# Layer 0's message sum: GpSimd's weighing is made to wait for VectorE's one-hots, and ScalarE makes the one-hots of every fourth group

## The reference, cut to what matters

```
        k_rel = jnp.einsum('nhd,rhde->rnhe', k, rel_att)
        v_rel = jnp.einsum('nhd,rhde->rnhe', v, rel_msg)
        key_e = k_rel[edge_type, edge_src]
        val_e = v_rel[edge_type, edge_src]
        att = (q[edge_dst] * key_e).sum(-1) * rel_pri[edge_type] / jnp.sqrt(jnp.float32(dk))
        ...
        w = ex / denom[seg]
        hsum = jax.ops.segment_sum(w[:, :, None] * val_e, seg, num_segments=S)
        cnt = jax.ops.segment_sum(jnp.ones((seg.shape[0],), x.dtype), seg, num_segments=S)
        t_rel = hsum.reshape(n, r, out_dim)
        present = cnt.reshape(n, r) > 0
        nrel = jnp.maximum(present.sum(-1), 1).astype(x.dtype)
        t = (t_rel * present[..., None].astype(x.dtype)).sum(1) / nrel[:, None]
```

## Time and profile before

| | us |
|---|---|
| median of 3 runs | 4695.33 |
| the 3 runs | 4687.55 to 4701.94 |
| the profiled execution | 4699.63 |
| its span, first to last instruction | 4697.9 |
| the sum's stretch, from the first one-hots (2364.1) to the last addition (2943) | 579 |

### The profile page before, as it was taken

The page is one execution under the profiler, slowest core; times in us unless marked ns, Lnnn a source line. Parts: engine busy times, 40 slices in busy tenths (PEclk is TensorE's granted clock), DMA queues, the critical chain, the costliest instruction groups (busy, mean ns, idle before and its releaser), DMA issues. The chain is left out here.

```text
span 4697.9 us, 56406 instructions
## 1 busy us (share of the span) xinstructions
PE 2830.0 (60%) x10793; PEld 1814.8 (39%) x10794; DVE 3034.3 (65%) x6076; ACT 1521.1 (32%) x3846; POOL 2074.6 (44%) x2102
## 2 busy tenths in 40 slices
PE   0799997666666665000077777666455566655653
PEld 0455554434334333000055555344234444444442
DVE  5333334555555555899889999666456666666657
ACT  0122222333333332322023333333243344334444
POOL 1000004777777776000033333222277777777751
PEclk9999998677776777555599999799677777777776
DMA  5344447999999998100056655000266666666652
GB/s 155 105 141 142 139 135 241 315 313 315 317 314 313 315 315 275 32 0 0 22 197 202 200 197 196 20 18 17 51 174 189 190 193 194 186 190 192 193 155 89
DMA packets 648049, 815.94 MB, mean 174 GB/s; under 512 B 155094, under 2 KB 552310, under 8 KB 647602
## 3 DMA queue, kind: packets, MB, share of 16 engines
q1 hardware_dynamic: 532228, 457.32, 30.5%
q0 software_dynamic: 115696, 357.28, 25.1%
HBM read 541.33 MB, written 274.25 MB: 174 GB/s over the span
## 5 line engine op out<-in xcount | busy, mean ns | idle before, releaser
L821 POOL DMA_INDIRECT rows<-kv,kvi x880 | 832.2, 946 | 889.6 <-DVEq L893 621.8
L1721 POOL DMA_INDIRECT g_rows<-x1t,srci x880 | 847.6, 963 | 286.8 <-issue 257.8
L866 PE MATMUL psD<-qs,hot 128*128 x1760 | 692.9, 520 | 271.1 <-DVE prod L907 201.9
L907 DVE TENSOR_TENSOR prod<-rows,psD 128x256 f32<-128x256 f32 x880 | 367.2, 418 | 458.8 <-DMA rows<-kv,kvi 335.5
L1875 PE MATMUL g_psM<-g_rows,g_hot 128*128 128x264 f32 x1760 | 567.7, 477 | 77.4 <-DVE g_rows L1993 68.1
L1157 POOL TENSOR_TENSOR wv<-vrows,wgt 128x1024 f32<-128x1024 f32 x110 | 217.4, 1976 | 839.0 <-DMA vrows<-val_v 598.8
L866 PEld LDWEIGHTS psD<-qs,hot 128*128 128x128 f32 x1760 | 382.5, 251 | 528.5 <-issue 312.6
L1237 PE MATMUL psM<-wv,vhot 128*128 128x260 f32 x1760 | 444.9, 396 | 137.5 <-DVE run L1256 130.7
L1875 PEld LDWEIGHTS g_psM<-g_rows,g_hot 128*128 128x128 f32 x1760 | 388.0, 232 | 170.7 <-issue 94.5
L886 ACT ACTIVATE off<-psB,npiota 128x256 f32<-128x256 f32 x440 | 207.8, 472 | 668.1 <-PE psB L857 666.8
L1237 PEld LDWEIGHTS psM<-wv,vhot 128*128 128x128 f32 x1760 | 317.5, 190 | 264.8 <-DVE run L1256 218.4
(11 more groups left out here) (364 smaller groups left out, 4629.7 us busy)
## 6 DMA issues: line engine op xcount, KB each, us to landing
val_v<-rows SPq DMA_DIRECT2D x220, 512.0 KB, 5.2
vrows<-val_v SPq DMA_DIRECT2D x220, 512.0 KB
kv<-stage SPq DMA_DIRECT2D x98, 768.0 KB, 4.7
sums_v<-g_run SPq DMA_DIRECT2D x110, 528.0 KB, 3.6
g_drow<-drow_v SPq DMA_DIRECT2D x55, 512.0 KB
rows<-kv,kvi POOLq DMA_INDIRECT x880, 4.9
g_rows<-x1t,srci POOLq DMA_INDIRECT x880
g_ndt<-nodeb SPq DMA_DIRECT2D x440, 6.0 KB
```

Of the source, the lines that this page charges most:

```text
L821: nc.gpsimd.indirect_dma_start(out=rows[:, k], out_offset=None, in_=table, in_offset=bass.IndirectOffsetOnAxis(ap=index[:, i * SLOTS + k:i ...
L866: nc.tensor.matmul(psD[:, k % 4, 0:cols], hot[:, t % 2, j * P:(j + 1) * P], node[:, ds(blk[t], 1)].rearrange("p o d -> p (o d)"), start=Tr ...
L907: ins = nc.vector.tensor_tensor(prod[:, k % 4], rows[:, k, 0:D], psD[:, k % 4, 0:D], ALU.mult)
L1721: nc.gpsimd.indirect_dma_start(out=rows[:, i % NBUF, k, 0:ROW1], out_offset=None, in_=dr["x1t"], in_offset=bass.IndirectOffsetOnAxis(ap=v[ ...
```

## The change

Three edits, all in `sum_messages`:

- **GpSimd** waits, ahead of each weighing, for `hot_done`: for group 1 until VectorE has made the one-hots of groups 0 and 1 of the same turn, for group 3 until it has made those of group 2.
- **ScalarE** makes the one-hots of group 3 (`places`, new tile `vfar`): |dr - iota| for each of the four slots, then 1 minus that, cut at zero. This stands in ScalarE's order behind the copies of visits 4 to 7 of the turn before and ahead of the copies for group 2. TensorE waits for them by `last_hot`.
- **VectorE** makes three one-hots in a turn rather than four, and its order is now: weigh(0), one-hots(0), one-hots(1), additions 4 to 7 of the turn before; weigh(2), one-hots(2), additions 0 to 3 of this turn.

```diff
                 def turn(i, first=False):
 
                     for g in range(NG):
+                        if g == 2:
+                            places(i)
                         beside(i, g)
...
+                def places(i):
+                    g = NG - 1
+                    for k in range(GS):
+                        ins = nc.scalar.activation(far[:, k], c["iota"][:], ACT.Abs, scale=-1.0, bias=v["dr"][:, ds(i * SLOTS + (g * GS + k), 1)])
+                    ins.then_inc(far_done, 1)
+                    act.wait_ge(far_done, i + 1)
+                    act.wait_ge(m_done, i * V8 + 2 * g + 2)
+                    nc.scalar.activation(hot[:, g * GS:(g + 1) * GS], far[:], ACT.Relu, bias=1.0, scale=-1.0).then_inc(last_hot, 1)
...
                     for g in range(1, NG, 2):
+                        pool.wait_ge(hot_done, i * (NG - 1) + min(g + 1, NG - 1))
                         weigh(pool, nc.gpsimd, i, g)
...
                         if t % 2 == 0:
-                            pe.wait_ge(hot_done, i * NG + t // 2 + 1)
+                            if t // 2 < NG - 1:
+                                pe.wait_ge(hot_done, i * (NG - 1) + t // 2 + 1)
+                            else:
+                                pe.wait_ge(last_hot, i + 1)
...
                 def turn(i, first=False):
-                    for g in range(NG):
-                        if g % 2 == 0:
-                            weigh(dve, nc.vector, i, g)
-                        dve.wait_ge(m_done, i * V8 + 2 * g + 2)
-                        nc.vector.tensor_tensor(hot[:, g * GS:(g + 1) * GS], c["iota"][:].unsqueeze(1).to_broadcast([P, GS, P]),
-                                                v["dr"][:, ts(i * NG + g, GS)].unsqueeze(2).to_broadcast([P, GS, P]),
-                                                ALU.is_equal).then_inc(hot_done, 1)
-
-                        if g >= 2:
-                            add(i, 2 * g - 4)
-                            add(i, 2 * g - 3)
+                    for g in range(0, NG, 2):
+                        weigh(dve, nc.vector, i, g)
+                        places(i, g)
+                        if g + 1 < NG - 1:
+                            places(i, g + 1)
+                        if g:
+                            for t in range(4):
+                                add(i, t)
                         elif not first:
-                            add(i - 1, 2 * g + 4)
-                            add(i - 1, 2 * g + 5)
+                            for t in range(4, V8):
+                                add(i - 1, t)
```

More of the change, by code:

```diff
@@ L1142, in sum_messages @@
         hot = sb("vhot", [P, SLOTS, P])
+        far = sb("vfar", [P, GS, P])
         run = sb("run", [P, V8, MSG])
@@ L1148, in sum_messages @@
         wv_done = [sem("wv_even_"), sem("wv_odd_")]
-        w_tr, w_out, ww_done, hot_done, m_done, run_done, kept = map(sem, (
-            "w_tr", "w_out", "ww_done", "vhot_done", "m_done", "run_done", "sum_kept"))
+        w_tr, w_out, ww_done, hot_done, far_done, last_hot, m_done, run_done, kept = map(sem, (
+            "w_tr", "w_out", "ww_done", "vhot_done", "vfar_done", "vhot_last", "m_done", "run_done", "sum_kept"))
         NG = SLOTS // GS
@@ L1257, in add, with places @@
                                                    in1=psM[:, t % 4, 0:width], op0=ALU.mult, op1=ALU.add).then_inc(run_done, 1)
-                def turn(i, first=False):
-                    for g in range(NG):
-                        if g % 2 == 0:
-                            weigh(dve, nc.vector, i, g)
-                        dve.wait_ge(m_done, i * V8 + 2 * g + 2)
-                        nc.vector.tensor_tensor(hot[:, g * GS:(g + 1) * GS], c["iota"][:].unsqueeze(1).to_broadcast([P, GS, P]),
-                                                v["dr"][:, ts(i * NG + g, GS)].unsqueeze(2).to_broadcast([P, GS, P]),
-                                                ALU.is_equal).then_inc(hot_done, 1)
-                        if g >= 2:
-                            add(i, 2 * g - 4)
-                            add(i, 2 * g - 3)
+                def places(i, g):
+                    dve.wait_ge(m_done, i * V8 + 2 * g + 2)
+                    nc.vector.tensor_tensor(hot[:, g * GS:(g + 1) * GS], c["iota"][:].unsqueeze(1).to_broadcast([P, GS, P]),
+                                            v["dr"][:, ts(i * NG + g, GS)].unsqueeze(2).to_broadcast([P, GS, P]),
+                                            ALU.is_equal).then_inc(hot_done, 1)
+                def turn(i, first=False):
+                    for g in range(0, NG, 2):
[6 more added lines that the diff above has]
+                                add(i, t)
                         elif not first:
-                            add(i - 1, 2 * g + 4)
-                            add(i - 1, 2 * g + 5)
+                            for t in range(4, V8):
+                                add(i - 1, t)
                 turn(0, True)
```

## The result

| | before | changed |
|---|---|---|
| median of 4 runs | 4698.18 us | 4620.92 us |
| lowest to highest | 4687.55 to 4701.94 | 4614.88 to 4624.22 |
| span of the profiled execution | 4697.9 us | 4622.5 us |

The ratio is 0.9841, with a 95% interval of 0.9822 to 0.9859: 1.6% faster, 75 us by the ratio and 75.4 by the spans.

The account below looks back on a forecast made before the run. VectorE's row of instructions was taken to bound the sum. Per turn 1.44 + 0.60 - 0.40 - 0.20 = 1.44 us; taken as 55 x 1.43 = 78.7 us off 4695.33, giving 4616.6 us, range 4594 to 4652.

Parts of the forecast that it names:

- Step 1: VectorE's one-hots in the sum: stalls behind GpSimd's weighings go if GpSimd runs beside additions alone, 1.44 us a turn saved.
- Step 2: VectorE's turn in the sum: one of four one-hots leaves VectorE, 0.60 us saved.
- Step 3: VectorE's four additions in a row: two seams become chained steps, costing 0.40 us a turn, and longer waits 0.20 more.
- The wait in another form: VectorE's additions: a third chained place where the wait takes another form, its step counted at 0.71 us.
- Step 4: GpSimd's weighing of 1.90 us fits beside four additions before VectorE's next weighing; nothing lost.
- L: Time from GpSimd's release by the one-hots until it starts: taken as 0.3 to 0.4 us, allowed 0.59 or 0.70.
- Steps 5 and 6: TensorE follows, working 8.08 us of a 9.06 turn; ScalarE's new work, 1.9 us a turn, costs nothing.
- The predicted loop of 7.5: ScalarE's copy and new work, TensorE's four visits and VectorE's addition: together 7.5 us against a turn of 9.06.
- Step 7: Single `vrows` loads behind GpSimd's weighing have 6.9 us against 5.5 for a pair; DMA share 0.68, cost nothing.

Follow-up runs that it names:

- The run with the wait last: Changed kernel with the three waits ahead of a VectorE addition reordered, the one for the addition before it (`run_done`) last: 4607.34 us, ratio 0.9815.
- the eight: Changed kernel with eight more \|dr - iota\| on ScalarE ahead of the four needed, written to a tile nobody reads: 4685.47 us, ratio 0.9955.

## Why the prediction was right, step by step

**The bound** was read rightly: VectorE's row of instructions is the stage, before and after; its only waits for anything are for its own additions.

**Step 1, the stalls, 1.44 a turn:** right in size, and the runs show that it was the order of VectorE that took them away. The prediction named GpSimd "now running beside additions alone" as the condition and left open what brings it about. The wait doesn't: without it nothing changes, and alone it costs 39 us. That the stalls go without it too was not foreseen in the prediction and is chance in part: loads and TensorE happen to let GpSimd go at the right time.

**Step 2, one one-hot, 0.60:** in the new order, 9.77 against 9.16, so 0.61. In the old order it was right too, but there the gain went again to a stall and a longer step. Two one-hots in a row, which no row had shown, take 1.21 with the step behind them, the 1.20 that was assumed.

**Step 3, the seams, 0.60 in all:** measured 0.71 (1.44 + 0.60 - 1.33). This is the one term that was a little small: the turn is 9.16 instead of 9.06, 5 us of 75. The wait in another form that I counted at 0.71 is the step of 0.77; the rest are hundredths of the other steps. The run with the wait last shows that the form of the wait, which step 3 only counted, sets the step through what stands behind it, and that 0.26 of this term needn't have been paid.

**Step 4, GpSimd's room:** L is 0.38 or so for group 1, against a room of 0.59, and 0.28 for group 3 (one-hots end at 2545.98, GpSimd starts at 2546.26), against 0.70. The estimate was 0.3 to 0.4. The run with the wait for the first addition, at a start of 0.85 behind it instead of 0.47, lost 0.17 a turn; the edge by the step is 0.59 + 0.08 = 0.67, and 0.85 is 0.18 beyond it.

**Steps 5 and 6, TensorE and ScalarE:** visit 0 starts 0.53 behind the first addition (predicted 0.54). TensorE's row and ScalarE's copy of the weights of group 2 in the changed kernel:

```profile
2546.68 0.19 ACT L1185 COPY wv<-wgt 128x16 f32 x1
2546.99 3.37 PEld L1253 LDWEIGHTS psM<-wv,vhot 128*128 128x128 f32 x16 [0.96 <-DVE run L1272]
2546.99 3.77 PE L1253 MATMUL psM<-wv,vhot 128*128 128x260 f32 x16 [0.56 <-DVE run L1272]
```

The copy ends at 2546.87, 5.15 behind the first addition (predicted 5.2), and visit 4 starts at 5.27 (predicted 5.3). The profile names an addition, that of 2545.90, as what TensorE waited for; by time it was ScalarE's copy, and in the kernel with four more distances the profile says so. The spare was there: 1.2 us more cost nothing. The predicted loop of 7.5 was somewhat long: 9.64 less the 2.34 that the eight take from start to start (2546.58 to 2548.92) is 7.3. The term that was too long is TensorE's. I took 2.02 for two visits twice, 4.04, and four visits in a row take 3.77, as the row above shows. In part for the same reason TensorE is busy for 85% and not the 89% that I expected.

**Step 7, the loads:** no long wait of GpSimd ends with a load in the changed kernel; in 2400 to 2830 all that are listed end with VectorE's one-hots. The DMA share became 0.74, not 0.68.

```profile
POOL wv L1158 <- DVE vhot L1276: 251.6, 94, 3.2
```

The forecast of 4616.6 was for 78.7 us less than the median then known, 4695.33. Against the median of the four runs before, 4698.18, the time fell by 77.3. The ratio's 75 us agrees within its noise with what the turn of 9.16 gives: 55 x 1.33 = 73. So the forecast had the sum 5 us too large for the reason of step 3, and the runs' scatter hid that.

## What to carry to other kernels

When GpSimd and VectorE share operands in SBUF, put VectorE's instructions that aren't stalled (here those with one of their two tensors in PSUM) into runs that are as long as one GpSimd instruction and its start delay, here 2.44 us for 1.90, and look in the trace where GpSimd starts: 1 us later all was lost. A wait that fixes GpSimd's start brought nothing where the run was long enough and GpSimd came at the right time by itself, and cost 39 us where the run was too short. Work taken off the busiest engine is worth its price only if the stalls don't reassemble: the same one-hots were worth 7 us in the old order and about 30 in the new. In a chain of dependent instructions put the wait for the predecessor last: what stood behind it was paid at the steps, 0.26 us of a turn of 9.16.

## What the runs showed of the hardware that I had not expected

A start of GpSimd that moved by 1.0 us against VectorE's row moved a stall from two instructions to one and kept its sum: 1.44 us in two before, 1.53 in one with ScalarE's part alone. And the same bytes took more of the DMA engines' time: 0.59 of 10.49 us a turn is 6.2, and 0.74 of 9.16 is 6.8, though no load came late. Without GpSimd's wait two of the loads go out together again (2548.94, as before in the earlier trace rows) and the share is 0.69, 6.3 us a turn; no run varied the spacing alone. TensorE's clock fell to a mean of 0.94 in a stretch where TensorE was still busy for 77% of the time (346.22 of 450), the same share at which it had been granted 1.00 before the change; a visible difference is that its idle time came in one piece of 2.4 us a turn rather than in four of up to 1. No run varied that alone, and other things differ between the two kernels, so the cause isn't shown.
